# A mixture-of-experts kernel: the first expert product over 128 columns for blocks of at most 128 rows

## The reference

```
logits = x @ Wg + bg
topk_scores, topk_idx = top_k(logits, 2); topk_scores = softmax(topk_scores)
h = tokens @ W1[e] + b1[e]                # 256 -> 1024
a = gelu(h) if e is even else silu(h)
y = a @ W2[e] + b2[e]                     # 1024 -> 256
out = sum over the row's two experts of score * y
x = layernorm(x + out)
```

## Time and profile before

| | before |
|---|---|
| median of 3 runs | 760.79 us (760.13 to 762.02) |
| profiled execution | 757.0 us, its span 755.3 us |
| mean granted TensorE clock | 0.913 |
| PE busy | 643.4 us, 85% |
| VectorE, ScalarE, GpSimd busy | 451.3, 393.1, 297.3 us |
| the stage of blocks | about 285 to 697 us |

### The profile page before, as it was taken

How to read it: one execution, slowest core, us unless ns; L and a number is a source line. 1 busy time by engine, 2 the same in 40 slices (tenths; PEclk the granted TensorE clock), 3 DMA queues, 4 the chain that set the end, 5 groups by cost and what they waited for, 6 DMA issues and landing times.

```text
span 755.3 us, 14636 instructions
## 1 busy us (share of the span) xinstructions
PE 643.4 (85%) x4472; PEld 600.1 (79%) x4472; DVE 451.3 (60%) x963; ACT 393.1 (52%) x715; POOL 297.3 (39%) x304
## 2 busy tenths in 40 slices
PE   5969799999967659899999999999999999998000
PEld 4858678788755558899999999999999999998000
DVE  4748889999997438455345454454454444442584
ACT  2555566576573132546455464563563645543474
POOL 5100116437446646227253182182531551112364
PEclk9998899999985669899999999999999999999555
DMA  8400222321223492933214123124141121101793
GB/s 254 125 28 1 83 68 74 105 91 65 91 84 120 146 296 56 300 129 113 89 43 155 51 90 114 41 62 144 36 155 51 30 58 44 44 20 33 256 298 125
DMA packets 57111, 78.71 MB, mean 104 GB/s; under 512 B 5190, under 2 KB 46611, under 8 KB 56884
## 3 DMA queue, kind: packets, MB, share of 16 engines
q1 hardware_dynamic: 41540, 51.59, 21.7%
q0 software_dynamic: 6496, 16.99, 6.5%
q10 hardware_dynamic: 8976, 8.72, 4.4%
HBM read 49.14 MB, written 28.92 MB: 103 GB/s over the span
## 4 chain that ended last, share of the span: by engine, by line
PE 73%; DVE 10%; issue 7%; ACT 4%; POOL 2%; DMA 2%; another core or an unknown queue 1%; SPq 0%; DVEq 0%; ACTq 0%; POOLq 0%
PE hT_ps L858 27%; PE y_ps L867 25%; PE vr_ps L711 7%; PE k_ps L711 6%; PE wo_ps L719 2%; PE xT_ps L876 2%; DVE o_all L1201 2%; PE small_ps L733 1%; DVE xl L1279 1%; DMA yy<-expert_out_dram 1%; POOL rstd_c L678 1%; PE xT_ps L779 1%; DVE nd L1208 1%; ACT L1006 1%
## 5 line engine op out<-in xcount | busy, mean ns | idle before, releaser
L858 PE MATMUL hT_ps<-xTh,wx 128*128 128x256 f32 x1120 | 215.3, 290 | 6.0 <-DVE aTl L1179 5.2
L867 PE MATMUL y_ps<-wx,aTh 128*128 128x256 f32 x1088 | 197.5, 283 | 0.9 <-DVE y_sb L1187 0.9
L858 PEld LDWEIGHTS hT_ps<-xTh,wx 128*128 128x128 f32 x1120 | 181.4, 196 | 6.9 <-DVE aTl L1179 5.4
L1179 DVE TENSOR_TENSOR aTl<-hT_ps,aTh 128x512 fp32r<-128x512 f32 x140 | 93.3, 689 | 143.2 <-ACT aTh L1069 139.7
L867 PEld LDWEIGHTS y_ps<-wx,aTh 128*128 128x128 f32 x1088 | 169.7, 192 | 1.2 <-issue 1.1
L659 POOL DMA_INDIRECT expert_out_dram<-y_sb,dest x70 | 68.2, 974 | 251.4 <-DVE y_sb L1187 235.6
L858 PE MATMUL hT_ps<-xTl,wx 128*128 128x256 f32 x560 | 160.9, 287 | 0.0
L867 PE MATMUL y_ps<-wx,aTl 128*128 128x256 f32 x544 | 154.0, 283 | 0.0
L1063 ACT ACT_TABLE_LOAD x33 | 42.3, 1283 | 170.5 <-PE hT_ps L858 161.8
L1063 ACT ACTIVATE hT_ps<-hT_ps,b_c 128x256 f32<-128x256 f32 x280 | 113.5, 468 | 30.4 <-PE hT_ps L858 23.3
L858 PEld LDWEIGHTS hT_ps<-xTl,wx 128*128 128x128 f32 x560 | 110.2, 197 | 0.0
(11 more groups left out here) (194 smaller groups left out, 852.8 us busy)
## 6 DMA issues: line engine op xcount, KB each, us to landing
staging<-in_L_ffn_W SPq DMA_DIRECT2D x16, 1024.0 KB
recs<-records_dram ACTq DMA_DIRECT2D x33, 258.0 KB, 2.8
yy<-expert_out_dram SPq DMA_DIRECT2D x16, 512.0 KB, 5.6
xin<-in_L_attn_x SPq DMA_DIRECT2D x16, 256.0 KB, 4.4
xres<-in_L_attn_x SPq DMA_DIRECT2D x16, 256.0 KB, 3.1
x_dram<-rec SPq DMA_DIRECT2D x16, 256.0 KB, 3.5
xx<-x_dram SPq DMA_DIRECT2D x2, 2048.0 KB
out<-res SPq DMA_DIRECT2D x16, 256.0 KB, 4.0
```

The source lines that it names most:

```text
L858: ins = pe.matmul(hT_ps[b][:, f, :], wx[:, s, part, off:off + P], xpart[t.slot % 2][:, cc, :], start=k == 0, stop=k == len(terms) - 1)
L867: ins = pe.matmul(y_ps[h], apart[t.slot % 2][:, fc, h * P:(h + 1) * P], wx[:, s, part, off:off + C], start=k == 0, stop=k == len(terms) - 1)
L1179: dve.tensor_tensor(aTl[u.slot % 2][:, 2 * b:2 * b + 2, :], hT_ps[b][:], aTh[u.slot % 2][:, 2 * b:2 * b + 2, :].bitcast(F32), ALU.subtract ...
```

## The change

`first_product` loads a second value, `full_t` of the block, and branches on it ahead of the parity. Where it is 0 (at most 128 rows), `product1` runs on 128 columns in place of 256, both in what it reads and in what it writes; otherwise as before. There are now four copies of `product1` in each block's code, two for each parity. The parts that come after still work on 256 columns; the upper 128 of them then hold what an earlier block left, and are never used.

```diff
-            def product1(t, s):
+            def product1(t, s, rows=BLK):
...
-                            ins = pe.matmul(hT_ps[b][:, f, :], wx[:, s, part, off:off + P], xpart[t.slot % 2][:, cc, :],
+                            ins = pe.matmul(hT_ps[b][:, f, 0:rows], wx[:, s, part, off:off + P], xpart[t.slot % 2][:, cc, 0:rows],
...
             def first_product(u):
+                full = pe.value_load(full_t[0:1, bass.ds(u.number, 1)], min_val=0, max_val=1)
                 expert = pe.value_load(ex_t[0:1, bass.ds(u.number, 1)], min_val=0, max_val=E - 1)
                 slot = expert % 2
                 pe.wait_ge(txl_done, u.upto(1))
                 pe.wait_ge(weights_ready, expert + 1)
-                with pe.If(slot == 0):
-                    product1(u, 0)
+                with pe.If(full == 0):
+                    with pe.If(slot == 0):
+                        product1(u, 0, P)
+                    with pe.Else():
+                        product1(u, 1, P)
                 with pe.Else():
-                    product1(u, 1)
+                    with pe.If(slot == 0):
+                        product1(u, 0)
+                    with pe.Else():
+                        product1(u, 1)
```

## The result

The change costs 5.3%: 801.0 us (796.1 to 804.9, 4 runs) against 760.5 us (758.3 to 762.0, 4 runs), ratio 1.053, 95% interval 1.049 to 1.057. The forecast was 796 us, range 778 to 820. The profiled execution took 799.6 us, its span 797.8; the mean granted clock was 0.902 where it had been 0.913.

What follows compares the result with a forecast made beforehand. The prediction took TensorE (PE) as the bound, its sequencer free only while PE's queue is full. Terms -0.7 + 1 + 30 + 1 + 4 = 35 us, on the median 760.8, gave 796 us, range 778 to 820.

Steps and rivals of the forecast that it cites:

- The mechanism: PE's program: pages of 256 instructions, each asked for on entering the one before; leaps over unrun copies stop PE.
- The sum of 35 us: Whole kernel: -0.7 narrower matmuls, +1 value and branch, +30 program fetch, +1 unused blocks, +4 clock.
- Pages: Ahead of first products: a block grows to 616 instructions, 2.41 pages, fetched late; 30 us lost, bounds 20 and 40.
- The walk: 616-instruction blocks followed page end by page end from 304 us: 13 stops of 0.6 to 3.7 us, 24 us added.
- Clock: After PE's new stops: three or four over 3 us, about half lowering the clock; 4 us lost, bounds 0 and 12.
- Value and branch: Sequencer ahead of first products: 0.9 us more, hidden except behind two short second products; 1.0 us lost, bounds 0 and 2.
- Narrow product: First products of blocks 16 and 20: 96 matmuls at 113 ns for 120; 0.7 us saved.
- Tail: Unused blocks 35 to 40: PE's leaps after its last product grow from 38 to 57 us; 1 us lost, bounds 0 and 7.
- pages several ahead: PE's program fetch runs many pages ahead, so the stops vanish: 761 to 766, say 763 us; chance 5%.
- Faster: First products of blocks 16 and 20: 96 matmuls at 60 ns save 5.8 us, no page late: 755 us; chance 3%.
- the short matmul is dear: 128-column matmuls of the short blocks take 213 ns each: 806 us; chance 6%.
- The clock falls at nearly every stop: At stops over 2 us, eight times, and the tail sets the end: some 818 us; chance 10%.

Runs made afterwards that it cites:

- static_narrow: Kernel before with the first products of blocks 16 and 20 written in as narrow, no added value, branch or copy: ratio 1.000 (0.999 to 1.002).
- dead2: Kernel before plus two never-run copies of the first product in each block, behind one more branch: 792.0 us, ratio 1.045.
- value_branch: Kernel before plus the table value and a branch on it ahead of each first product, no more copies: ratio 1.014 (1.008 to 1.019).
- dead4: Kernel before plus four never-run copies of the first product in each block, jumped over in one branch: 893.8 us, ratio 1.173.
- vb_one: Kernel before plus table value and branch, that value loaded behind the previous block's first product, the expert's load left in place: ratio 1.002 (1.000 to 1.005).

## Why the prediction was right

**The mechanism** held as written: program pages, one at a time, and leaps. The sum of 35 us is best checked from the start of block 3's first product to PE's last matmul, 383.7 us before (313.45 to 697.14) and 420.1 after (318.09 to 738.21): +36.4 us in the two profiled executions, where the terms said 35. The other 6.1 us of the two spans' 42.5 lie before (4.6, of them 2.1 before the first expert matmul) and behind (1.5); static_narrow, which costs nothing, starts block 3 at 318.96, so this is spread between executions. The profiled one of before was 3.8 us under its median, as the prediction says. That the sum comes so near is luck in part: the pages came 5 us under their term, and the clock 4 us and the value and branch 3 us over theirs.

**Pages: 30 forecast, 25.1 measured.** In 14 of the 16 stops the sequencer (in two that lie within a product, PE itself) goes on 1.3 to 1.5 us behind the end of a packet of q8. The other two, 0.4 us that ends where this stretch begins and 0.7 us at 504.22, have no packet that fits. The 14 add 21.93 us to the 1.5 of before, in 12 more places. Each costs 0.26 us beyond its own length, since the first piece behind it takes 6.01 or 6.02 us for 5.75, as in the earlier trace rows: 12 x 0.26 = 3.12, in sum 25.05 us. The walk gave 13 stops of 0.6 to 3.7 us with 24 us in sum; 16 came, the longest of 3.62. q8 moved 103 packets, as said; the 58 of them between 384 and 688 us are 2.3 a block, where 2.4 was said. dead2 puts pages, clock and its one branch together at 34 us, the sum of the two forecasts.

**Clock: 4 forecast, 8.2 measured.** Windows behind two of the stops (us; busy us of PE, its loads, DVE, ACT, POOL, each with its count; granted clock; DMA share; GB/s):

```profile
546.60:550.10 3.50, 3.50 (x19) 3.50 (x18) 0.00 (x0) 1.02 (x1) 0.00 (x0) 0.51 0.02 5
587.60:594.40 6.80, 5.16 (x24) 5.16 (x25) 0.00 (x0) 2.10 (x3) 0.00 (x0) 0.50 0.06 22
```

A clock of 0.51 and 0.50 is 1.2 GHz, the lower level. There are five such stretches behind 313 us, four of 3.4 us and this one of 6.8, and 88 matmuls lie in them at 213 ns where 120 would do: 88 x 93 ns = 8.2 us. I had looked for falls behind stops of over 3 us, three or four of them, and in half of those; only one stop was over 3 us. They came behind stops of 1.9, 2.8, 2.6, 3.6 and 2.7 us, and not behind one of 2.8 at 357: five of the six longest. My row had a gap of 3.28 us, and I let its length stand for the least that does it; no row said so.

**Value and branch: 1 forecast, 3.9 measured here, 10 by themselves.** This is the step that failed, though the whole came out. The prediction says: "PE starts that product at 397.31: 1.28 us ahead. It shrinks to some 0.4 us." The 397.31 is the start of the chain's piece. The first matmul starts 0.25 us earlier, at 397.06, because the chain gives the transposes their time up to their end. The lead at that block was 1.03 us, and the median of all is 0.96. The added 0.65 + 0.25 leaves 0.06 of it, and 0.06 us is the lead at which PE has run dry; the new branch takes more than that, 345 ns in the median where such branches take some 200. In the changed kernel 25 of 28 first products start with a lead of 0.06 us. What it costs there is what is left of the 36.4, with all else that is in the remainder: 36.4 - 25.1 - 8.2 + 0.8 = 3.9 us, outside the term's bounds of 0 and 2. Of it the stop at 504.22, behind a short second product, is 0.66 + 0.26 = 0.9 us; this is the place where the prediction looked for 0.5. By value_branch it is 10 us when nothing else stops PE, and dead2 and value_branch add up to 44 us against the change's 40. It would fit that part of it lies within the stops, since a lead that is used up makes each late page later by as much; no run takes this apart.

**Narrow product: -0.7 forecast, -0.8 measured.** At block 16 of the changed kernel:

```profile
482.36 0.44 PE xT_ps L876 x4
482.79 5.36 PE hT_ps L858 x48
488.15 5.80 PE y_ps L867 x48
```

```profile
L858 PE MATMUL hT_ps<-xTh,wx 128*128 128x128 f32 x64 | 11.1, 276 | 0.0
```

The 48 start 113 ns apart (5.30 us from the first to the last), and L733 with 8 columns gave 113: between 8 and 128 columns the time doesn't depend on them. That the weight load sets it fits this, but no run changes the load. The Trainium skill, "TensorE: Matmul & The Clock Gate", section "Back-to-back issue gap", has some 81 ns for 128 columns; these 32-bit weights do not reach it.

**Tail: 1 forecast, 0 measured.** PE's drain and POOL's, in the changed kernel:

```profile
L121 PEldq DRAIN  x1: 73/73/73, 784.1 to 784.1; - x1
...
L121 POOLq DRAIN  x1: 7223/7223/7223, 790.4 to 790.4; - x1
```

PE drains 45.9 us behind its last matmul, 57 had been worked out, and POOL's end is still the later one. The unused blocks' pages came faster than the 4.9 us each that I took, though the longest branch there took 6.4.

The rivals: *pages several ahead* is out by dead2, and with it the 128 KiB of instruction memory as something that would help here (128 KiB is eight of these packets); of the two statements in the Trainium skill, "Runtime: NRT & Kernel Launch", section "Instruction fetch mechanics", the two lines of 16 KiB are the one that these runs bear out, with packets of 16 KB and, as the stops are read here, one page ahead at most. That pages which are leapt over come in as well (dead4, 129 packets) neither statement says. *Faster* and *the short matmul is dear* are out by static_narrow. *The clock falls at nearly every stop* came near to being true, five falls against the eight it asked for, but at 8.2 us, not 21.

Open: what makes a page take 3 us and more, of which its packet is 1 us. The stop at 543.53 shows how the time is divided: the branch at L885 goes over one page end (437 ns, from 542.65), the packet moves from 543.86 to 544.74, and the branch at L891 gets over the next end at 546.25, 1.5 us behind the packet. What takes the 1.2 us ahead of the packet and the 1.5 behind it no run shows. Open too is whether the changed kernel with one value moved, as in vb_one, would win back its part, which was not run. None of the versions beats the kernel before.

## What to carry to other kernels

A branch that picks between written-out copies costs on TensorE by the code that it leaps over, run or not: before adding one, count the block's instructions in pages of 256 (16 KB) and look how long the longest branch of the kernel takes where it crosses one. A gain of 7 ns on 96 matmuls doesn't pay for 30 pages. And before adding scalar work to a busy engine's sequencer, measure for each product the time from the last branch's end to the first matmul's start, on the timeline and not on the chain: up to that much is free, and the budget ahead of one product can't be spent at another.

## What the runs showed of the hardware that I had not expected

- Moving two loads (1.28 us of sequencer time) to a seemingly idle place won nothing, 1.020 for 1.014, and moving one made it free, 1.002.
- The granted clock halved behind a stop of 1.9 us and at four of the five stops from 2.6 us on. A stretch of 3.4 us cost 1.5 us (a product of 7.50 us for 6.01); the one of 6.8 us began 1.6 us before its stop ended and cost 2.3 us (8.29 for 6.01).
- The profile put four stops of PE down to VectorE that were its own sequencer's; the branch rows showed it.
- Every stop costs TensorE 0.26 us more than its length.
- Unused blocks' code that is leapt over is fetched too: the packets are the pages of the program, within 3 in 132.
- The median of one and the same kernel was 749.8 us on one chip and 759 to 761 on others, 1.4% apart: more than most of the effects here, and only ratios within a session showed them.
